# A fused attention and feed-forward kernel: GpSimd multiplies the heads' sums by reciprocals that VectorE writes to SBUF, and V's scale is applied at the second stage's residual add

## What is computed

```python
q, k, v = heads(query @ Wq + bq), heads(key @ Wk + bk), heads(values @ Wv + bv)
scores = einsum('bhqd,bhkd->bhqk', q, k) / sqrt(32)
scores = where(j < i, scores, -1e30)
attn = softmax(scores); attn[:, :, 0, :] = 0
ctx = einsum('bhqk,bhkd->bhqd', attn, v)
x = layer_norm(query + ctx @ Wo + bo, ln1_g, ln1_b)
out = layer_norm(x + relu(x @ W1 + b1) @ W2 + b2, ln2_g, ln2_b)
```

## Time and profile before

| | |
|---|---|
| median of 3 runs | 2656.55 us (2653.86 to 2657.02) |
| the profiled execution, its own time | 2657.73 us |
| its span | 2655.6 us |
| busy: PE | 2504.5 us, 94% |
| busy: PEld | 1887.0 us, 71% |
| busy: DVE | 2108.4 us, 79% |
| busy: ACT | 1628.1 us, 61% |
| busy: POOL | 1569.9 us, 59% |
| chain that ended last, by engine | PE 58%, POOL 25%, issue 12%, DVE 3%, ACT 1% |

### The profile page before, as it was taken

How to read it: one execution, slowest core, us unless ns; L and a number is a source line. 1 busy time by engine, 2 the same in 40 slices (tenths; PEclk the granted TensorE clock), 3 DMA queues, 4 the chain that set the end, 5 groups by cost and what they waited for, 6 DMA issues and landing times.

```text
span 2655.6 us, 62848 instructions
## 1 busy us (share of the span) xinstructions
PE 2504.5 (94%) x22664; PEld 1887.0 (71%) x22664; DVE 2108.4 (79%) x4871; ACT 1628.1 (61%) x2881; POOL 1569.9 (59%) x1721
## 2 busy tenths in 40 slices
PE   4899999999999999978999999999999999999998
PEld 1455555555555555557888888888888888888887
DVE  7999999999999999789767677776767676767675
ACT  2788888899999889877343434343434344444433
POOL 2677777777777777667555555554554555454543
PEclk9999999999999999989999999999999999999999
DMA  5344444443334333346132222222222222222220
GB/s 170 110 116 119 116 115 109 115 106 103 98 99 104 103 105 97 89 130 173 49 69 49 65 51 68 53 66 55 62 59 57 65 57 64 57 65 56 65 57 25
DMA packets 444455, 225.03 MB, mean 85 GB/s; under 512 B 302368, under 2 KB 388192, under 8 KB 444144
## 3 DMA queue, kind: packets, MB, share of 16 engines
q1 hardware_dynamic: 442544, 219.71, 32.3%
q10 hardware_dynamic: 1600, 1.31, 0.2%
HBM read 112.36 MB, written 57.69 MB: 64 GB/s over the span
## 4 chain that ended last, share of the span: by engine, by line
PE 58%; POOL 25%; issue 12%; DVE 3%; ACT 1%; DMA 0%; POOLq 0%; ACTq 0%; SPq 0%; DVEq 0%
PE h_ps L1652 25%; POOL prob_lo L494 24%; PE acc L1668 22%; PE front L1638 6%; PE lin_ps L935 2%; PE o_ps L977 1%; PE max_ps L908 1%; DVE W L1609 1%; PE st_ps L957 1%; PE lin_ps L931 0%; POOL scan L509 0%; POOLq L83 0%; PE st_ps L992 0%; ACTq L570 0%; PE o_ps L979 0%
## 5 line engine op out<-in xcount | busy, mean ns | idle before, releaser
L494 POOL TENSOR_TENSOR prob_lo<-probs,prob_hi 128x512 f16<-128x512 f32 (+1 forms) x768 | 793.0, 1040 | 347.8 <-ACT prob_hi L581 313.4
L1652 PE MATMUL h_ps<-x_halves,W 128*128 128x256 f16 x6144 | 754.9, 273 | 2.4 <-ACT hf L1442 2.4
L1668 PE MATMUL acc<-W,hs 128*128 128x256 f16 x5376 | 669.6, 273 | 0.0
L1652 PEld LDWEIGHTS h_ps<-x_halves,W 128*128 128x128 f16 x6144 | 595.8, 98 | 87.2 <-issue 15.3
L1442 ACT ACTIVATE hf<-h_ps,b1s,scale_evac 128x256 f32<-128x256 f32 x512 | 284.7, 562 | 575.1 <-PE h_ps L1652 573.1
L1668 PEld LDWEIGHTS acc<-W,hs 128*128 128x128 f16 x5376 | 526.0, 98 | 60.9
L1367 POOL TENSOR_TENSOR hf<-hf 128x256 f32<-128x256 f32 x256 | 238.5, 932 | 498.4 <-ACT hf L1442 498.4
L587 ACT ACTIVATE probs<-st_ps,exp_scale 128x512 f32<-128x512 f32 (+1 forms) x768 | 467.0, 608 | 106.7 <-PE st_ps L992 84.9
L887 DVE CUSTOM_DVE_ANT_0 max_ps<-max_ps,mask_q 128x256 f32<-128x256 f32 (+2 forms) x768 | 418.9, 561 | 76.4 <-PE max_ps L908 75.5
L581 ACT ACTIVATE prob_hi<-probs 128x512 f16<-128x512 f32 (+1 forms) x768 | 427.3, 556 | 22.4 <-issue 7.2
L1605 DVE TENSOR_TENSOR hs<-hf,hs 128x896 f16<-128x896 f32 x256 | 279.9, 1113 | 141.4 <-ACT hs L1431 141.4
(11 more groups left out here) (151 smaller groups left out, 3550.1 us busy)
## 6 DMA issues: line engine op xcount, KB each, us to landing
heads<-stage SPq DMA_DIRECT2D x748, 64.0 KB, 2.1
raw_c<-in_cT SPq DMA_DIRECT2D x64, 256.0 KB, 3.2
raw_x<-in_xT SPq DMA_DIRECT2D x64, 256.0 KB, 4.4
o_in<-ctx_rows SPq DMA_DIRECT2D x256, 64.0 KB, 2.5
x_in<-in_x SPq DMA_DIRECT2D x32, 512.0 KB, 3.9
x_rows<-x SPq DMA_DIRECT2D x64, 256.0 KB, 2.1
o_in<-x_rows SPq DMA_DIRECT2D x256, 64.0 KB, 2.5
out<-y SPq DMA_DIRECT2D x32, 512.0 KB, 3.0
```

Of the source, the lines that this page charges most:

```text
L494: pool.tensor_tensor(prob_lo[:, k % 4, 0:w], probs[:, k % PROBS, 0:w], prob_hi[:, k % 4, 0:w], ALU.subtract).then_inc(pl_done, 1)
L1652: last = pe.matmul(h_ps[:, f % 2, 0:T], W1[:, aw, j, f * P:(f + 1) * P], x1_halves[:, item.parity, aa, j, :], start=(j == 0 and m == 0), s ...
L1668: last = pe.matmul(acc_products[:, n, :], hs[:, p % HS, aa, n, :], W2[:, p, aw, n, :], start=(p == 0 and m == 0 and n % 2 == 0), stop=(p = ...
```

## The change

- Line 807 goes away on VectorE. In its place GpSimd multiplies `osum` by the reciprocals, one tensor_tensor with the reciprocals broadcast over a head's 32 columns, in slot PV_AT + 3h + 4, ahead of that slot's `prob_lo`.
- VectorE's reciprocal is written to a new SBUF tile `sums` instead of back to `o_ps`. `osum` and `sums` get two buffers; VectorE's reduction of head h waits for GpSimd's product of head h - 2.
- TensorE's first product of head h + 2 waits for VectorE's reciprocal of head h (`o_step`) and no longer for `onorm`.
- `value_scale` is kept for all 16 sequences and is applied in the second stage: the residual add becomes (front * value_scale) + x.
- In `ranges`, `exp_scale` is made by two tensor_tensor in place of one scalar_tensor_tensor; there are seven steps instead of six.

```diff
@@ -241,7 +242,8 @@
         maxima = sb("maxima", [P, 2, QT, 4], F32)
         negmax_parts = sb("negmax_parts", [P, 2, 4, QT], F16)
         rows = sb("rows", [P, 2, 32], F16)
-        osum = sb("osum", [P, QT, HD], F32)
+        osum = sb("osum", [P, 2, QT, HD], F32)
+        sums = sb("sums", [P, 2, QT], F32)
         onorm = sb("onorm", [P, 2, QT, 4, HD], F32)
         bias = sb("bias", [P, 2, GROUPS], F32)
         identb = sb("identb", [P, P], BF16)
...
@@ -271,7 +273,7 @@
         inverse = sb("inverse", [P, 3, 2], F32)
         act_bias = sb("act_bias", [P, 3, 2, GROUPS], F32)
         exp_scale = sb("exp_scale", [P, 3], F32)
-        value_scale = sb("value_scale", [P, 3], F32)
+        value_scale = sb("value_scale", [P, B], F32)
 
         lin_ps = held.enter_context(nc.psum_tensor("lin_ps", [P, 2, 512], F32))
         max_ps = held.enter_context(nc.psum_tensor("max_ps", [P, 2, 512], F32))
...
@@ -460,9 +462,9 @@
 
     def gpsimd(pool):
 
-        zeros = osum[:, 0:2, :].rearrange("p q d -> p (q d)").bitcast(BF16)
+        zeros = osum[:, 0, 0:2, :].rearrange("p q d -> p (q d)").bitcast(BF16)
         pool.memset(onorm[0:B, 0, :, :, :].rearrange("p q h d -> p (q h d)"), 0.0).then_inc(consts, 1)
-        pool.memset(osum[:, 0:2, :], 0.0).then_inc(consts, 1)
+        pool.memset(osum[:, 0, 0:2, :], 0.0).then_inc(consts, 1)
         pool.wait_ge(consts, 2)
         pool.memset(heads_at[96:98, :, 1, :, :], ONES).then_inc(consts, 1)
         pool.wait_ge(consts, 3)
...
@@ -487,6 +489,18 @@
 
         for window in range(B + BACK):
             for s in range(SLOTS):
+                for h in range(HEADS):
+                    t, i = h // 4, h % 4
+                    for item, _ in due(window, s, SLOTS, B, PV_AT + 3 * h + 4):
+                        wait_for(pool, o_step, 2 * HEADS, item, 2 * h + 2)
+                        if i == 0:
+
+                            wait_for(pool, stored[t % 2], 64, item, 32 * (t // 2))
+                            if t == 0 and item.n == 0:
+                                pool.wait_ge(first_rows, 16)
+                        pool.tensor_tensor(onorm[:, t % 2, :, i, :], osum[:, h % 2, :, :],
+                                           sums[:, h % 2, :].unsqueeze(2).to_broadcast([P, QT, HD]), ALU.mult
+                                           ).then_inc(o_out, 1)
                 for item, k in due(window, s, SLOTS, B, ST_AT, SLOTS):
                     w = ST_WIDTH[k % 3]
                     wait_for(pool, ph_done, SLOTS, item, k + 1)
...
@@ -685,11 +699,13 @@
                               ).then_inc(range_step, 1)
             dve.wait_ge(range_step, base + 2)
             dve.reciprocal(inverse[:, at, :], power[:, at, :]).then_inc(range_step, 1)
-            dve.scalar_tensor_tensor(out=exp_scale[:, at:at + 1], in0=power[:, at, 0:1], scalar=exp_unit[:, :],
-                                     in1=power[:, at, 1:2], op0=ALU.mult, op1=ALU.mult).then_inc(range_step, 1)
-            dve.tensor_tensor(value_scale[:, at:at + 1], power[:, at, 0:1], value_unit[:, :], ALU.mult
+            dve.tensor_tensor(exp_scale[:, at:at + 1], power[:, at, 0:1], power[:, at, 1:2], ALU.mult
                               ).then_inc(range_step, 1)
-            dve.wait_ge(range_step, base + 3)
+            dve.tensor_tensor(value_scale[:, item.n:item.n + 1], power[:, at, 0:1], value_unit[:, :], ALU.mult
+                              ).then_inc(range_step, 1)
+            dve.wait_ge(range_step, base + 4)
+            dve.tensor_tensor(exp_scale[:, at:at + 1], exp_scale[:, at:at + 1], exp_unit[:, :], ALU.mult
+                              ).then_inc(range_step, 1)
             dve.tensor_tensor(act_bias[:, at, :, :], scaled_bias[:, :, :],
                               inverse[:, at, :].unsqueeze(2).to_broadcast([P, 2, GROUPS]), ALU.mult
                               ).then_inc(range_step, 1)
...
@@ -785,29 +801,14 @@
                     dve.tensor_reduce(bounds.top[:, :], scan[:, 0, :].rearrange("p (r c) -> p c r", c=4), AX_X, ALU.max
                                       ).then_inc(bounds.kept, 1)
                 for h in range(HEADS):
-                    t, i = h // 4, h % 4
                     o = o_ps[:, h % 2, 0:QT * VW].rearrange("p (q w) -> p q w", w=VW)
                     for item, _ in due(window, s, SLOTS, B, PV_AT + 3 * h + 3):
                         wait_for(dve, pv_done, SLOTS, item, 3 * h + 3)
-                        wait_for(dve, o_out, HEADS, item, h)
-                        dve.tensor_reduce(osum[:, :, :],
+                        wait_for(dve, o_out, HEADS, item, h - 1)
+                        dve.tensor_reduce(osum[:, h % 2, :, :],
                                           o[:, :, 0:2 * HD].rearrange("p q (c d) -> p q d c", c=2),
                                           AX_X, ALU.add).then_inc(o_step, 1)
-                        dve.reciprocal(o[:, :, 2 * HD], o[:, :, 2 * HD]).then_inc(o_step, 1)
-                    for item, _ in due(window, s, SLOTS, B, PV_AT + 3 * h + 4):
-                        wait_for(dve, o_step, 2 * HEADS, item, 2 * h + 2)
-                        if i == 0:
-
-                            wait_for(dve, stored[t % 2], 64, item, 32 * (t // 2))
-                            if t == 0 and item.n == 0:
-                                dve.wait_ge(first_rows, 16)
-                        if h == 0:
-                            dve.wait_ge(*ranged(item, 5))
-                        at = item.n % 3
-                        dve.scalar_tensor_tensor(out=onorm[:, t % 2, :, i, :], in0=osum[:, :, :],
-                                                 scalar=value_scale[:, at:at + 1],
-                                                 in1=o[:, :, 2 * HD].unsqueeze(2).to_broadcast([P, QT, HD]),
-                                                 op0=ALU.mult, op1=ALU.mult).then_inc(o_out, 1)
+                        dve.reciprocal(sums[:, h % 2, :], o[:, :, 2 * HD]).then_inc(o_step, 1)
                 for t in range(GROUPS):
 
 
...
@@ -967,7 +968,7 @@
                 if k == 0:
                     wait_for(pe, lin_out, len(UNITS), item, V_READY)
                 if c == 0:
-                    wait_for(pe, o_out, HEADS, item, h - 1)
+                    wait_for(pe, o_step, 2 * HEADS, item, 2 * h - 2)
                 wait_for(pe, pl_done, SLOTS, item, k + 1)
                 for m, (kt, at) in enumerate(ST_UNITS[c]):
                     for q in range(kt, QT):
...
@@ -1014,6 +1015,9 @@
 
     programs = Programs(sync, gpsimd, scalar, vector, tensor)
     programs.full_slots = SLOTS * B
+    programs.sequences = B
+    programs.value_scale = value_scale
+    programs.values_ranged = (range_step, RANGE_STEPS * (B - 2) + RANGE_VALUE)
     programs.row_stores = 32 * GROUPS // 2
     programs.inputs_read = (lin_step, SLOTS * B)
     programs.splits_done = (lo_done, NCHUNK * B)
...
@@ -1545,7 +1549,12 @@
 
                         wait_for(dve, y_part, 6, item, 2 - 12)
                         tile = x1[:, item.parity, u, :]
-                        dve.tensor_tensor(tile, front[:, u, :], x_in[:, u, :], ALU.add).then_inc(res_done, 1)
+                        if item.n == 0 and u == 0:
+                            dve.wait_ge(*before.values_ranged)
+                        sequence = item.n // (CHUNKS // before.sequences)
+                        dve.scalar_tensor_tensor(out=tile, in0=front[:, u, :],
+                                                 scalar=before.value_scale[:, sequence:sequence + 1],
+                                                 in1=x_in[:, u, :], op0=ALU.mult, op1=ALU.add).then_inc(res_done, 1)
                         wait_for(dve, res_done, U, item, u + 1)
                         if item.n == 0 and u == 0:
                             dve.wait_ge(front_loaded, 16 * len(FRONT_VECTORS))
```

11 lines of the change are left out of this document (6 added, 5 removed).

## The result

| | before | after |
|---|---|---|
| median | 2655.98 us (2653.86 to 2657.02, 4 runs) | 2677.46 us (2671.52 to 2683.09, 4 runs) |
| the profiled execution, its own time | 2657.73 us | 2671.52 us |
| its span | 2655.6 us | 2669.7 us |
| busy: DVE | 2108.4 us | 2035.1 us |
| busy: POOL | 1569.9 us | 1670.8 us |

The ratio is 1.0077, with an interval of 1.0064 to 1.009. The changed kernel is slower by 0.8%; the forecast was 0.4% faster, and the measured time lies outside its range. The four runs scatter over 12 us, those of before over 3. The profiled one is the fastest of the four, so its trace shows 14 us of a loss that is 21.5 us in the median.

What follows compares the result with a forecast made beforehand. TensorE was taken as the bound, with VectorE close behind in the attention. Terms of -21.8, +9.8, +3.2 and -1.6 us give -10.4: 2647.3 from the profiled 2657.7, less 1.2 for the median, 2646 us; range 2631 to 2668.

Steps and rivals of the forecast that it cites:

- The product's length: GpSimd's new product of sums and reciprocals was taken at 0.46 us, from line 1370's similar instruction.
- VectorE's relief: Six removed line 807 instructions free 1.56 us a sequence, less 0.2 us for blocking: -21.8 us over 16 sequences.
- the stretch: Third of each period (716.8 to 743.5 us) where VectorE works almost without pause and TensorE waits 1.8 us for it.
- Rival D: GpSimd's products and VectorE's low parts block each other, which takes the gain: 2654 us, chance 0.07.
- The tight units: Even 512-column units whose prob_lo is barely in time; the product delays units 4, 34, 46: 0.61 us a sequence, +9.8 us.
- The mixing: In eight windows where GpSimd also mixes W2, product and additions share gaps: 0.4 us each, +3.2 us.
- The changeover: TensorE waits for the earlier reciprocal instead of onorm, there and at one more such place: -1.6 us.
- The second stage: The residual add costs VectorE 3.6 us more, under a TensorE busy without a break, so nothing.
- Rival C: Slower: the product delays every tight unit, +12 us, 2668 us, chance 0.17.
- A's half-way case: Half the gain if all TensorE's attention waits on VectorE go (2625 us in full): 2635 us; that rival's chance 0.12.
- C's product by the gaps alone: Product length from which the delays at three narrow GpSimd gaps outweigh VectorE's 1.36 us gain: 0.69 us.
- GpSimd's forecast: GpSimd's busy time in the attention, 100 to 1080 us, rises from 722 to about 840 of 980 us, 86%.

Runs made afterwards that it cites:

- e12: Kernel before with only V's scale moved to the second stage, the product staying on VectorE with its second operand in o_ps: 2655.6 us, 0.9994.
- e9: Changed kernel with GpSimd's five additions of the W2 mixing three slots earlier: 2653.6 us, 0.9992.
- e10: Kernel before with GpSimd's five additions of the W2 mixing three slots earlier, as a control: 2647.4 us, 0.9967.
- e14: Changed kernel with the mixing's additions three slots earlier and VectorE's second low part of x one slot later: 2649.9 us, 0.9968.
- e17: e14 with the loads of raw_c also issued ahead of the fourth group's twelve copies: 2647.1 us, 0.9955.
- e11: Changed kernel with the loads of raw_c issued ahead of the fourth group's twelve copies: 2677.3 us, 1.0086.
- e18: Kernel before with the mixing's additions three slots earlier and the loads of raw_c early: 2646.6 us, 0.9953.

## Why the forecast was wrong, step by step

**The product's length** was right: 0.46 forecast, 0.402 median. Its mean is 0.503 us, since it is held up where VectorE works from SBUF. The Trainium skill's factor of two against VectorE (*GPSIMD Engine Reference*, § Engine selection) isn't borne out at this size: 402 ns beside 339 for line 807, and 1.4 times the 279 of the same form in e12.

**VectorE's relief** (-21.8 us) is the largest term that failed, and with it the sign: even with the mixing cured in both kernels (e9 and e10) the changed one is 6 us slower. The forecast took the waits of the stretch as VectorE's and let 1.36 us a sequence through to TensorE. TensorE's waits for the maxima in a plain period fell from 1.8 to 1.4 us, where below 0.6 had been named as the sign of being right. VectorE did come sooner, and met two things. At unit 10 its low part of x now starts ahead of `prob_lo` and not behind it, so that it is GpSimd that is held up. Of the changed kernel, VectorE, GpSimd and TensorE:

```profile
737.42 0.74 DVE L609 SCALAR_TENSOR_TENSOR acts<-raw_x,inverse,acts 128x512 f16<-128x512 f32 x1
```

```profile
737.54 2.28 POOL L508 TENSOR_TENSOR prob_lo<-probs,prob_hi 128x512 f16<-128x512 f32 x2 [0.17 <-ACT prob_hi L595]
```

```profile
739.24 0.20 PE L978 MATMUL o_ps<-V,prob_hi 128*128 128x65 f16 x1 [0.55 <-POOL prob_lo L508]
```

In the kernel before, `prob_lo` went first and the low part paid (1.57 us instead of 0.74), which cost TensorE 0.06 us at unit 10:

```profile
722.66 2.24 POOL L494 TENSOR_TENSOR prob_lo<-probs,prob_hi 128x512 f16<-128x512 f32 x2 [0.65 <-ACT prob_hi L581]
```

```profile
722.79 1.57 DVE L595 SCALAR_TENSOR_TENSOR acts<-raw_x,inverse,acts 128x512 f16<-128x512 f32 x1
```

The pairs' lengths hardly differ. What differs is their first instruction, unit 10's: it takes 1.66 us in the chain above, where an undisturbed one takes 1.16. And behind that, at unit 16, stands the load of raw_c (e14, e17). A plain window gained nothing; it lost 0.4 us. Rival D had named this blocking and put it at 8 us, at the products and at VectorE's low parts.

**The tight units** (+0.61 us a sequence) were right in kind. Unit 34 went from 0.06 to 0.17 us (0.16 forecast), unit 46 from 0.38 to 0.74 (0.30 forecast); unit 4 from 0.35 to 0.70 (0.15 forecast), since the product is stretched just there and the `prob_lo` behind it starts late. GpSimd in the changed kernel, beside the earlier trace rows:

```profile
727.89 0.85 POOL L501 TENSOR_TENSOR onorm<-osum,sums 128x128 f32<-128x128 f32 x1
728.70 1.15 POOL L508 TENSOR_TENSOR prob_lo<-probs,prob_hi 128x512 f16<-128x512 f32 x1
```

Unit 10 (0.06 to 0.55 us) wasn't among those counted. Together about 1.3 us a sequence instead of 0.61. The blocking itself was foreseen (0.2 us of VectorE's gain); that the loser changes with which of the two starts first was not.

**The mixing** (+3.2 us) is where most of the measured loss sits: +13.4 us in the profiled run's seven full windows, of which some 3 us are the plain windows' 0.4 us and some 3 us the two falls of the clock. The forecast added 0.4 us for GpSimd's gaps and dismissed the stores in one sentence, "issued more than ten slots before". That looked at GpSimd's wait for the stores, and not at SyncE's wait for GpSimd, nor at what stands behind the stores in SyncE's queue. The additions' end, the stores and the rows are one chain, and what hid its end was the 1.4 us by which `onorm` held TensorE at unit 18. The change took that wait away and with it the cover.

**The clock** had no term. Waits of some 2 us sit where it sometimes falls, each fall 1.5 us more; by the mean clocks, and by e11's trace, it seems to make most of the difference between the profiled run's 14 us and the median's 21.5.

**The changeover** (-1.6 us) did not come out: from the last sequence's first unit to its last it is 86.6 us instead of 86.4. TensorE's two waits for `onorm` there (6.4 us) are 1.1 us for the reciprocal, but those for `prob_lo` rose from 11.4 to 16.3 us. The window ahead of it is 3.0 us shorter, and there a wait of 1.97 us for `onorm` is gone; but in e10, e12 and e18, which keep the product on VectorE, the same window takes 70.5, 69.2 and 74.0 us at clocks of 0.98, 1.00 and 0.95, so what of the 3.0 us is the change's is not shown. That the two come close to the forecast together is luck.

**The second stage** (nothing) is 2.4 us longer after the last unit, which the forecast had named as a sign of being wrong. TensorE's busy time there is the same (1427.2 and 1426.9 us), and the add takes 743 ns, close to the 738 forecast. e12, with 3.1 us there and an unchanged whole, speaks against a loss by itself; why TensorE pauses longer there stays open.

Rival C had the sign, and not the mechanism. Three numbers of the working don't follow from their own terms, and none touches the sum: A's half-way case is 2635 us and not the range's end of 2631, C's product by the gaps alone is 0.71 us and not 0.69, and the stretch holds some 227 of the 256 products, which makes GpSimd's forecast 826 us and not 840 (measured 796).

## What to carry to other kernels

Before a wait is removed, ask what it covers: list, for the engine that will arrive sooner, everything else that it takes from queues near that place, and read each one's slack from the timeline, the DMA queue's among them. A producer that is moved or delayed holds the whole in-order queue that waits for it, so price what stands behind the wait. Here both were one case: the wait that covered the late rows was itself a loss, and moving the additions was worth 9 us without the change. When two engines share a path, which of them starts first decides who pays, and a tenth of a microsecond can turn it round.
